# 512-column products for the small tiles, kept rotary tables and a split tail in an attention and expert block

## The chip, the cores and the metric

The kernel runs on one core of a Trainium2 chip. Its time is the device time of one launch in microseconds; the median of three runs before is 1562.0 us (1560.15 to 1563.43). A core has five engines with queues of their own: TensorE (PE; its weight loads are shown apart as PEld), VectorE (DVE), ScalarE (ACT), GpSimd (POOL) and SyncE (SP), which here only issues DMAs.

## What is computed

The block takes x of 2048 tokens by 256 features, normalises it, and adds attention and a mixture of experts to it. All of it is float32.

```python
xn = layernorm(x)
q, gate, k, v = split(xn @ w_qkv.T)          # 16 heads, 4 key/value heads, D = 128
q, k = rope(layernorm(q)), rope(layernorm(k))
attn = softmax(causal(q @ k.T / sqrt(D)))    # each k, v serves 4 heads
out = ((attn @ v) * sigmoid(gate)) @ w_o.T
w_tok = top-2 of 8 experts by softmax(xn @ w_router)
ffn = sum over experts of w_tok * (relu(xn @ w_fc) ** 2 @ w_proj)
result = x + out + ffn
```

## The kernel before

The work goes through four groups g (one key/value head and its HG = 4 query heads each) and within each through 16 tiles t of 128 tokens. Tile t attends to t + 1 key tiles, so tiles 0 to 7 are small and 8 to 15 large. Exact float32 products are made of three fp32r products each (`three`, L1279): high by high, high by low, low by high. So each operand that TensorE takes is first split: ScalarE copies it as the high part (`_hi`), VectorE subtracts for the low part (`_lo`).

For a tile the steps are: products `Q`, `KV`, `G` (gate); ScalarE's `q_take` and `kv_take` out of PSUM; the rotary part (`tables` on GpSimd from cosines and sines; `sumsq`, `same` on VectorE, `swap` and `rstd` on GpSimd, `rope_b` on VectorE); transposes `QT` and `KT` (L1339, L1343); the scores of each head in chunks of up to 512 keys; `max` on VectorE, `exp` on ScalarE into `probs`. Then the probabilities of a pair p of two heads are transposed, two key tiles i at a time: four blocks of 128 columns into a `pt_bank` (`turn_probs`, L1361), `p_hi` (L939), `p_lo` (L1219), and the value products `pv` of 256 columns into `o_bank`, a half of the bank for each pair. `turn_probs` step n waits for `p_lo` of step n - 2, since there are two `pt_bank`s. Then `o_take` per pair (L948), the transposed gate `GT` (L1382), `og` (L1234), `og_hi` (L957), `og_lo` (L1238), `OUT` (12 products, L1390) and `out_add` (L1243).

A tile with an odd number of key tiles ends with a half-wide step for each pair. The 23 expert slots run between the tiles from some 350 us on (`XS`, `H`, `Y`, with `xs_load`, `fc_load`, `pj_load` and `y_store` on SP; `y_store` waits for ScalarE's `y_take`).

At the start x is loaded in four parts of four tiles (`stats`, `x_rstd`, `norm`, then transposes `XT`, L1299, and `xT_lo`). The weights of a group come in two halves c, whose query part is centred (L1115 to L1119) and split (`wq_lo`, L1127); that of the gate is split by `wg_lo`.

What sets the order: `plan_program` (L334) places all steps on the five engines one by one, by assumed costs and a due time per step, from the tables `BEGIN` (one number for each tile and pair) and `DUE` (an offset for each kind of step). Each engine then works its list strictly in order, waiting on semaphores.

Of the kernel before, what the change touches and what calls it, by code (L numbers as in the profile page):

```python
# [38 lines left out]
P = 128  # L39
# [28 lines left out]
GATHER_AT, GATHER_EVERY = 440, 3  # L68
FILLS = (NSLOT + 1) // 2
ROUTE_PARTS = ((0, E), (E, E + E * E), (E + E * E, E + E * E + NSLOT), (E + E * E + NSLOT, 2 * E + E * E + NSLOT))  # L70
# [14 lines left out]
BEGIN = [26.59, 41.38, 29.62, 36.09, 25.65, 50.81, 47.59, 46.92, 64.18, 72.49, 75.23, 89.37, 102.35, 116.24,  # L85
# [10 lines left out]

DUE = {"qkv": -43.81, "rope": -12.53, "turn": -314.72, "v_lo": -91.35, "gate": 7.24, "inv": -214.95,
       "turn_gate": 4.73, "og": 4.02, "out": 10.53, "out_add": 1.16, "scores": -12.47, "max": -5.95,
       "exp": 18.26, "prob_step": 1.95, "pv": 7.99, "p_hi": -283.79, "p_lo": -1.72, "moe": 348.73,
       "moe_step": 36.0, "moe_evict": -19.57, "route": 89.48, "x1": 11.16, "x2": 38.95, "x3": 39.51,  # L100
       "logits": -17.39, "gate_w": -102.68, "scatter": 143.34, "next_w": -59.05, "wo": 575.69, "comb": 73.3,
       "window": 0.02}
# [18 lines left out]

def due_times():


    begin = {}
    for g in range(G):
        for t in range(T):
            for p in range(HG // 2):
                begin[g, t, p] = BEGIN[(g * T + t) * 2 + p]
    for g in range(G):  # L130
        begin[g, T, 0] = begin[g, T, 1] = begin[g + 1, 0, 0] if g + 1 < G else BEGIN[-1]
    return begin


def prob_order():


    return [(g, t, p, i) for g in range(G) for t in range(T) for p in range(HG // 2) for i in range((t + 2) // 2)]


def program_steps():
# [17 lines left out]
    for q in range(4):  # L159
        add("sp", ("x_load", q), 0.5, [], 0, 512)  # L160
        if q == 0:
# [3 lines left out]
        if q == 1:  # L165
# [9 lines left out]
    quarter = [0.0, DUE["x1"], DUE["x2"], DUE["x3"]]  # L175
    for q in range(4):
        add("dve stats", ("stats", q), 1.75, [("x_load", q)], quarter[q])
        add("pool x", ("x_rstd", q), 1.4, [("stats", q), ("pool_consts",)], quarter[q] - 5)
        add("dve norm", ("norm", q), 1.4, [("x_rstd", q)], quarter[q])
        for c in range(CT):  # L180
            i = 2 * q + c
            add("pe XT", ("XT", i), 0.44 if q else 1.06, [("norm", q), ("ident_load",)], quarter[q] + 2)
            add("act XT", ("xT_hi", i), 0.48, [("XT", i)], quarter[q] + 2)
            add("dve XT", ("xT_lo", i), 0.6, [("xT_hi", i)], quarter[q] + 2)
        add("pe L", ("L", q), 1.4, [("xT_lo", 2 * q + 1), ("wr_lo",)], quarter[q] + DUE["logits"])
        add("act L", ("logit_copy", q), 0.48, [("L", q), ("LT", q - 1) if q else None], quarter[q] + DUE["logits"])
        add("pe L", ("LT", q), 0.25, [("logit_copy", q)], quarter[q] + DUE["logits"] + 1)
        add("dve logit", ("route", q), 0.2, [("LT", q)], quarter[q] + DUE["logits"] + 1)
# [16 lines left out]
    for g in range(G):  # L205
# [20 lines left out]
        for t in range(T):  # L226
            b0, b1, b2 = begin[g, t, 0], begin[g, t, 1], begin[g, t + 1, 0]
            t1, t2 = tile_before(g, t), tile_before(g, t, 2)
            n_t = g * T + t
            if n_t >= 2:  # L230
                add("sp angles", ("angle_load", g, t), 0.45, [old(t2, "tables")], b0 + DUE["rope"] - 15, 64)
            add("pool rope", ("tables", g, t), 4.0, [old(t1, "rope_b"), old(t1, "same"), ("angle_load", g, t),
# [206 lines left out]
def build(nc, x, w_in, w_o, q_w, q_b, k_w, k_b, w_router, w_fc, w_proj, cos_sin, ident, mask_in, route_const, out):  # L439
# [9 lines left out]
    with ExitStack() as ctx:  # L449
# [3 lines left out]
        def sem(name):  # L453
            return ctx.enter_context(nc.semaphore(name))
# [1010 lines left out]
```

## Time and profile before

| | us |
|---|---|
| median of 3 runs | 1562.0 |
| the profiled execution | 1561.02 |
| its span, first to last instruction | 1559.2 |
| TensorE busy | 1508.5 |
| VectorE busy | 1310.9 |
| ScalarE busy | 1154.7 |
| GpSimd busy | 523.9 |
| end of the value products of tile 7, group 0 | 173.9 |
| end of the value products of tile 15, groups 0, 1, 2, 3 | 410.3, 805.9, 1191.9, 1551.4 |

Busy times are of one profiled execution. A matmul's end is modelled and overlaps the next one's start, so for a row of matmuls the distance between starts is their price, and TensorE's idle time is a lower bound of what it lost. The mean granted clock of TensorE is 0.996 of its full level.

### The profile page before, as it was taken

How to read it: one execution, taken by the hardware profiler on the slowest of the kernel's cores; microseconds unless marked ns; L12 is line 12 of the kernel's file. 1: busy time of each engine (PE TensorE's matmuls, PEld its weight loads, DVE VectorE, ACT ScalarE, POOL GpSimd, SP SyncE). 2: the span in 40 equal slices, each digit the busy share in tenths (PEclk: the TensorE clock that was granted, in tenths of full speed). 3: DMA queues.
4: the chain of work that ended last, by engine and by line, in shares of the span. 5: the costliest groups of instructions: out<-in, count | busy, mean ns of one | idle time of the engine just before them, and what ended most of it. 6: DMA issues, size and time to landing. Idle time of an engine off the chain costs nothing.

```text
span 1559.2 us, 29914 instructions
## 1 busy us (share of the span) xinstructions
PE 1508.5 (97%) x10589; PEld 1380.0 (89%) x10589; DVE 1310.9 (84%) x3011; ACT 1154.7 (74%) x3013; POOL 523.9 (34%) x726
## 2 busy tenths in 40 slices
PE   4999999999899999999999999999999999999998
PEld 3788999999899999999898999999998998899998
DVE  7999888787898888788789888887779988888875
ACT  3777777777778787787778777777777776776775
POOL 5544434320553222121046331221105535343200
PEclk9999999999999999999999999999999999999999
DMA  4400010001111000101211000110111101102000
GB/s 139 142 5 21 21 42 23 21 28 50 45 33 30 32 30 29 32 26 39 66 45 40 25 25 11 47 31 30 28 46 45 33 13 31 30 20 66 16 8 8
DMA packets 46646, 56.65 MB, mean 36 GB/s; under 512 B 4576, under 2 KB 43232, under 8 KB 46304
## 3 DMA queue, kind: packets, MB, share of 16 engines
q1 hardware_dynamic: 43424, 46.34, 9.5%
q0 software_dynamic: 3072, 8.39, 1.7%
q8 instruction: 84, 1.38, 0.4%
q14 instruction: 66, 0.54, 0.1%
HBM read 42.40 MB, written 18.35 MB: 39 GB/s over the span
## 4 chain that ended last, share of the span: by engine, by line
PE 74%; DVE 17%; ACT 5%; issue 2%; POOL 1%; DMA 1%; SPq 0%; DVEq 0%; ACTq 0%; POOLq 0%
PE bank L1286 39%; PE o_bank L1286 19%; PE pt_bank L1361 12%; DVE pT_lo L1219 3%; DVE neg_chunk_max L1205 2%; DVE t_same L1169 2%; DVE bank L1202 2%; PE bank L1339 1%; PE bank L1382 1%; DVE t_same L1165 1%; ACT probs L920 1%; DVE sumsq L1137 1%; DVE t_same L1153 1%; ACT gate L930 1%; ACT pT_hi L939 1%
## 5 line engine op out<-in xcount | busy, mean ns | idle before, releaser
L920 ACT ACTIVATE probs<-bank,neg_max 128x512 f32<-128x512 f32 (+3 forms) x640 | 399.8, 634 | 91.7 <-DVE neg_max L1212 57.6
L1219 DVE TENSOR_TENSOR pT_lo<-pt_bank,pT_hi 128x512 fp32r<-128x512 f32 (+1 forms) x576 | 368.7, 654 | 100.7 <-ACT pT_hi L939 96.8
L939 ACT ACTIVATE pT_hi<-pt_bank 128x512 fp32r<-128x512 f32 (+1 forms) x576 | 325.8, 578 | 131.3 <-PE pt_bank L1361 81.6
L1286 PE MATMUL o_bank<-pT_hi,v_hi 128*128 128x256 f32 x1088 | 333.7, 307 | 2.9 <-DVE pT_lo L1219 1.9
L1361 PE MATMUL pt_bank<-ident_f,probs 128*128 128x128 f32 x2176 | 315.2, 273 | 10.5 <-DVE pT_lo L1219 10.0
L785 POOL TENSOR_TENSOR t_swap<-qk_raw,table_swap 128x256 f32<-128x256 f32 (+1 forms) x256 | 135.4, 560 | 561.9 <-ACT t_same L889 560.9
L1286 PE MATMUL o_bank<-pT_hi,v_lo 128*128 128x256 f32 x1088 | 307.3, 282 | 0.0
L1286 PE MATMUL o_bank<-pT_lo,v_hi 128*128 128x256 f32 x1088 | 306.5, 282 | 0.0
L1205 DVE TENSOR_REDUCE neg_chunk_max<-bank 128x1 f32<-128x512 f32 (+1 forms) x384 | 244.8, 650 | 49.2 <-PE bank L1286 48.1
L1361 PEld LDWEIGHTS pt_bank<-ident_f,probs 128*128 128x128 f32 x2176 | 252.2, 140 | 36.0 <-DVE pT_lo L1219 13.5
L1286 PE MATMUL bank<-kT_hi,qT_hi 128*128 128x512 f32 (+3 forms) x640 | 244.0, 381 | 2.7 <-ACT probs L920 2.3
L1286 PE MATMUL bank<-kT_lo,qT_hi 128*128 128x512 f32 (+3 forms) x640 | 231.3, 361 | 0.0
L1286 PE MATMUL bank<-kT_hi,qT_lo 128*128 128x512 f32 (+3 forms) x640 | 231.1, 361 | 0.0
L1286 PEld LDWEIGHTS o_bank<-pT_hi,v_hi 128*128 128x128 f32 x1088 | 206.7, 190 | 9.9 <-DVE pT_lo L1219 4.7
L1286 PEld LDWEIGHTS o_bank<-pT_lo,v_hi 128*128 128x128 f32 x1088 | 207.2, 190 | 2.0
L1286 PEld LDWEIGHTS o_bank<-pT_hi,v_lo 128*128 128x128 f32 x1088 | 206.0, 189 | 0.0
L1286 PE MATMUL bank<-w_hi,xT_hi 128*128 128x512 f32 (+1 forms) x384 | 144.0, 375 | 3.9 <-DVE oT L1234 1.5
L1286 PEld LDWEIGHTS bank<-kT_hi,qT_hi 128*128 128x128 f32 x640 | 121.3, 189 | 19.3 <-ACT probs L920 6.9
L1286 PE MATMUL bank<-w_lo,xT_hi 128*128 128x512 f32 (+1 forms) x384 | 137.6, 358 | 0.0
L1286 PE MATMUL bank<-w_hi,xT_lo 128*128 128x512 f32 (+1 forms) x384 | 137.3, 358 | 0.0
L920 ACT ACTIVATION_READ_ACCUMULATOR probs<-bank,neg_max 128x1 f32 x640 | 137.1, 214 | 0.0
L1286 PEld LDWEIGHTS bank<-kT_hi,qT_lo 128*128 128x128 f32 x640 | 120.7, 189 | 17.0
(163 smaller groups left out, 2974.6 us busy)
## 6 DMA issues: line engine op xcount, KB each, us to landing
rows<-xs SPq DMA_DIRECT2D x23, 256.0 KB, 2.7
expert_raw<-in_w_fc SPq DMA_DIRECT2D x23, 256.0 KB, 3.0
expert_raw<-in_w_proj SPq DMA_DIRECT2D x23, 256.0 KB, 2.7
yb<-rows SPq DMA_DIRECT2D x23, 256.0 KB, 2.1
xs<-in_x SPq DMA_DIRECT2D x11, 512.0 KB, 4.9
w_raw<-in_w_in SPq DMA_DIRECT2D x7, 640.0 KB, 4.3
angles<-in_cos_sin SPq DMA_DIRECT2D x64, 64.0 KB, 1.9
acc<-in_x SPq DMA_DIRECT2D x4, 512.0 KB, 8.3
```

Of the source, the lines that this page charges most:

```text
L785: ins = pool.tensor_tensor(t_swap[:, heads, to], qk_raw[:, heads, of], table_swap[:, i:i + 1, to].to_broadcast([P, count, 64]), ALU.mult)
L920: act.activation(probs[:, u, h % 2, first:first + width], bank("scores", g, t, h, c)[:, 0:width], ACT.Exp, bias=neg_max[:, u, h % 2:h % 2 ...
L930: ins = act.activation(gh, gh, ACT.Identity, bias=inv, scale=inv)
L939: act.activation(pT_hi[:, n % PT_RING, 0:width], pt_bank[n % 2][:, 0:width], ACT.Copy)\
L1137: dve.tensor_reduce(sumsq[:], squares[:], AX.X, ALU.add).then_inc(sumsq_done, 1)
L1153: dve.tensor_tensor(t_same[:, 0:HG, :], qk_raw[:, 0:HG, :], table_same[:, 0:1, :].to_broadcast([P, HG, D]), ALU.mult).then_inc(same_done, 1)
L1169: ins = dve.scalar_tensor_tensor(rotated[:, h, :], t_same[:, h, :], rstd[:, h:h + 1], table_bias[:, h // HG, :], ALU.mult, ALU.add)
L1202: ins = dve.tensor_tensor_reduce(scores, scores, mask[:, CHUNK - width:CHUNK], 1.0, least, ALU.add, ALU.min, to)
L1205: ins = dve.tensor_reduce(to, scores, AX.X, ALU.min)
L1219: dve.tensor_tensor(pT_lo[:, n % PT_RING, 0:width], pt_bank[n % 2][:, 0:width], pT_hi[:, n % PT_RING, 0:width].bitcast(F32), ALU.subtract) ...
L1286: ins = pe.matmul(out_ap, s, m, start=(start and done == 1), stop=(stop and done == last))
L1361: ins = pe.transpose(pt_bank[n % 2][:, (2 * jj + hh) * P:(2 * jj + hh + 1) * P], probs[:, p, hh, j * P:(j + 1) * P], ident_f[:])
```

## The change

It has these parts.

- Tiles below SMALL = 8 handle all four heads together: a `turn_probs` step is one key tile of four heads, and `pv` is 512 columns wide, one step per key tile. `probs` is laid out by t % 2 there. `o_take` is one copy of 512 columns.
- The rotary tables are made by GpSimd in group 0 only; SP stores each (384 KB) to DRAM, and in groups 1 to 3 SP loads it back, into `made_tables` or into `norm_rows` (the table of norm weights, no longer needed), by t % 2.
- x is loaded in five parts, of 1, 3, 4, 4 and 4 tiles, and the first tile's two transposes go together.
- The last tile's `og`, `og_hi`, `og_lo` and `OUT` are done in two halves of two heads.
- `BEGIN` has 192 more numbers, three shifts for each tile, and nearly all numbers of `BEGIN` and `DUE` differ; the assumed costs follow the new widths. Scratch areas at the start lie elsewhere.

```diff
-GATHER_AT, GATHER_EVERY = 440, 3
+GATHER_AT, GATHER_EVERY = 428, 3
+SMALL = 8
+X_PARTS = ((0, 1), (1, 4), (4, 8), (8, 12), (12, 16))
...
-BEGIN = [26.59, 41.38, 29.62, 36.09, 25.65, 50.81, 47.59, 46.92, 64.18, 72.49, 75.23, 89.37, 102.35, 116.24,
+BEGIN = [15.02, 7.63, 57.3, 43.4, -9.53, -4.16, 15.06, 12.59, 36.85, 79.37, 35.75, 29.31, 53.04, 75.64, 82.97,
...
+def shift(g, t, k):
+    return BEGIN[2 * G * T + 1 + 3 * (g * T + t) + k]
...
+def head_groups(t):
+    return [range(HG)] if t < SMALL else [range(0, 2), range(2, 4)]
+def prob_blocks(t, i):
+    return [i] if t < SMALL else [j for j in (2 * i, 2 * i + 1) if j <= t]
+def prob_count(t):
+    return t + 1 if t < SMALL else (t + 2) // 2
...
+def probs_held(g, t, u):
+    if t < 2:
+        return (g - 1, T - 1, u, prob_count(T - 1) - 1) if g else None
+    if t < SMALL:
+        return g, t - 2, 0, prob_count(t - 2) - 1
+    if t == SMALL:
+        return g, SMALL - 2 + u, 0, prob_count(SMALL - 2 + u) - 1
+    return g, t - 1, u, prob_count(t - 1) - 1
...
+            if g == 0:
...
+                add("pool rope", table, 4.0, [old(t1, "rope_b"), old(t1, "same"), ("angle_load", g, t), ("ln_tables",),
+                                              ("table_store", t - 1) if t else None], b0 + DUE["rope"])
+                add("sp tables", ("table_store", t), 0.45, [table], 0, 384)
+            else:
+                table = ("table_load", g, t)
+                free = [("tables", 0, T - 1)] if (g, t) == (1, 0) else [old(t2 if n_t != T + 1 else t1, "rope_b")]
+                add("sp tables", table, 0.45, free + [("table_store", T - 1)], b0 + DUE["rope"] - DUE["table"], 384)
...
+        def rotary(g, t):
+            return made_tables if g == 0 or t % 2 else norm_rows
+        def wait_tables(w, g, t):
+            if g == 0:
+                w.wait_ge(tables_done, t + 1)
+            else:
+                w.wait_ge(tables_back[t % 2], 16 * (((g - 1) * T + t) // 2 + 1))
+        def prob_cols(t, h, first, width):
+            if t < SMALL:
+                return probs[:, t % 2, h * SMALL * P + first:h * SMALL * P + first + width]
+            return probs[:, h // 2, h % 2 * S + first:h % 2 * S + first + width]
...
+                elif kind == "table_store":
+                    w.wait_ge(tables_done, a[0] + 1)
+                    sp.dma_start(kept_tables[a[0]], made_tables[:]).then_inc(tables_kept, 16)
+                elif kind == "table_load":
...
+                        w.wait_ge(rotated_done, n - 1 if n > T + 1 else T)
+                    sp.dma_start(rotary(g, t)[:, 0:3], kept_tables[t]).then_inc(tables_back[t % 2], 16)
...
-                    width = 256 * min(2, t + 1 - 2 * i)
+                    width = P * len(head_groups(t)[p]) * len(prob_blocks(t, i))
...
-                    for jj in range(min(2, t + 1 - 2 * i)):
-                        for hh in range(2):
-                            j = 2 * i + jj
-                            ins = pe.transpose(pt_bank[n % 2][:, (2 * jj + hh) * P:(2 * jj + hh + 1) * P],
-                                               probs[:, p, hh, j * P:(j + 1) * P], ident_f[:])
+                    for k, (j, h) in enumerate((j, h) for j in blocks for h in heads):
+                        ins = pe.transpose(pt_bank[n % 2][:, k * P:(k + 1) * P], prob_cols(t, h, j * P, P), ident_f[:])
...
-                    for jj in range(min(2, t + 1 - 2 * i)):
-                        j, cols = 2 * i + jj, slice(2 * jj * P, 2 * (jj + 1) * P)
-                        ins = three(o_bank[:, 256 * p:256 * p + 256], [(v_hi[:, j, :], v_lo[:, j, :])],
+                    wide = P * len(head_groups(t)[p])
+                    for k, j in enumerate(prob_blocks(t, i)):
+                        cols = slice(k * wide, (k + 1) * wide)
+                        ins = three(o_bank[:, head_cols(t, p)], [(v_hi[:, j, :], v_lo[:, j, :])],
...
+                elif kind == "OUT_rest":
+                    g, t = LAST_TILE
+                    w.wait_ge(og_lo_done, g * T + t + 2)
+                    heads = range(HG // 2, HG)
```

Three places in the order of the instructions. The first is the start of VectorE's list. Before, `w_raw` and `probs` hold the two halves of the weights of group 0.

```order
L1023 TENSOR_SCALAR xn<-acc,probs 128x256 x4
L1127 TENSOR_TENSOR w_lo<-w_raw,w_hi 128x768
L1115 TENSOR_REDUCE head_sum<-probs 128x5
L1117 TENSOR_SCALAR head_mean<-head_sum 128x5
L1119 TENSOR_TENSOR probs<-probs,head_mean 128x640
L1029 TENSOR_TENSOR xT_lo<-bank,xT_hi 128x512
L1009 TENSOR_TENSOR wr_lo<-probs,wr_hi 128x16
L1029 TENSOR_TENSOR xT_lo<-bank,xT_hi 128x512
L1127 TENSOR_TENSOR w_lo<-probs,w_hi 128x768
```

Now, where `routing_rest` holds the second half of the weights:

```order
L1140 TENSOR_TENSOR wr_lo<-late_keys,wr_hi 128x16
L1145 BN_STATS late_keys<-acc 128x6 x3
L1148 BN_AGGR late_keys<-late_keys 128x2 x3
L1145 BN_STATS late_keys<-acc 128x6 x4
L1148 BN_AGGR late_keys<-late_keys 128x2 x4
...
L1257 TENSOR_TENSOR w_lo<-routing_rest,w_hi 128x768
...
L1154 TENSOR_SCALAR xn<-acc,late_keys 128x256 x11
L1288 TENSOR_TENSOR v_lo<-bank,v_hi 128x128
```

The 768-wide `w_lo` of the second half, for which the first Q product waits, stands behind the statistics of three more parts of x, and eleven normalisations stand between it and the first rotary step.

The second place is TensorE's list in an early small tile, tile 1 of group 0: transposition of probabilities and value products, before.

```order
L1361 MATMUL pt_bank<-ident_f,probs 128x128 x4
L1339 MATMUL bank<-ident_f,t_same 128x128 x4
L1286 MATMUL o_bank<-pT_hi,v_hi 128x256
L1286 MATMUL o_bank<-pT_lo,v_hi 128x256
L1286 MATMUL o_bank<-pT_hi,v_lo 128x256
```

Now the same tile, between scores of tile 2 (384 keys):

```order
L1421 MATMUL bank<-kT_hi,qT_lo 128x384
L1421 MATMUL o_bank<-pT_hi,v_hi 128x512
L1421 MATMUL o_bank<-pT_lo,v_hi 128x512
L1421 MATMUL o_bank<-pT_hi,v_lo 128x512
L1421 MATMUL bank<-kT_hi,qT_hi 128x384
```

Each key tile has three products of 512 columns in place of three for each of two pairs; the transposes of the tile's two key tiles, eight in a row, stand well ahead, with the rotary transposes and the projections of later tiles between.

The third place is the end of TensorE's list, before.

```order
L1286 MATMUL o_bank<-pT_hi,v_lo 128x256
L1382 MATMUL bank<-ident_f,gate 128x128 x4
L1286 MATMUL bank<-wo_hi,ogT_hi 128x256
L1286 MATMUL bank<-wo_lo,ogT_hi 128x256
L1286 MATMUL bank<-wo_hi,ogT_lo 128x256
```

Now:

```order
L1421 MATMUL bank<-wo_hi,ogT_hi 128x256
L1421 MATMUL bank<-wo_lo,ogT_hi 128x256
L1421 MATMUL bank<-wo_hi,ogT_lo 128x256
L1421 MATMUL o_bank<-pT_hi,v_hi 128x256
L1421 MATMUL o_bank<-pT_lo,v_hi 128x256
L1421 MATMUL o_bank<-pT_hi,v_lo 128x256
```

The gate's transposes have left the end, and the first six of the twelve OUT products stand ahead of the last six value products; six OUT products are left behind them.

## Rows read from the trace of the kernel before

**Rows 1.** The page: span, and TensorE's busy time (first entry, with share and instructions).

```profile
span 1559.2 us, 29914 instructions
...
PE 1508.5 (97%) x10589; PEld 1380.0 (89%) x10589; DVE 1310.9 (84%) x3011; ACT 1154.7 (74%) x3013; POOL 523.9 (34%) x726
```

**Rows 2.** Busy time by stretch; the first number is its length, then by engine.

```profile
core 0: us, PE busy (x) PEld busy (x) DVE busy (x) ACT busy (x) POOL busy (x), PEclk, DMA share, GB/s
0.00:20.00 20.00, 4.94 (x15) 2.63 (x16) 11.60 (x26) 5.50 (x9) 7.15 (x18) 1.00 0.68 200
20.00:60.00 40.00, 32.28 (x182) 24.61 (x182) 37.85 (x112) 24.29 (x67) 28.06 (x40) 0.96 0.29 98
60.00:120.00 60.00, 56.92 (x405) 50.72 (x404) 55.75 (x150) 43.64 (x124) 27.39 (x40) 1.00 0.16 55
...
410.00:548.00 138.00, 134.98 (x951) 124.61 (x950) 121.56 (x296) 108.90 (x289) 59.35 (x84) 0.99 0.11 34
...
1192.00:1327.00 135.00, 130.36 (x898) 118.34 (x896) 121.53 (x294) 103.52 (x281) 69.16 (x94) 1.00 0.09 25
1327.00:1551.00 224.00, 221.41 (x1570) 203.48 (x1569) 185.91 (x407) 158.80 (x415) 61.12 (x79) 1.00 0.08 25
```

**Rows 3.** The waits of all engines: us in total, times, longest us.

```profile
POOL table_same L769 <- DVE t_same L1169: 218.0, 59, 6.8
...
PE pt_bank L1361 <- DVE pT_lo L1219: 10.0, 16, 2.1
...
PE bank L1286 <- DVE xT_lo L1029: 8.9, 3, 6.1
...
PE bank L1339 <- DVE t_same L1169: 4.7, 8, 2.1
```

**Rows 4.** Timeline of TensorE near 1201 and 1223 us: start, length, instruction.

```profile
1201.12 0.28 PE L1286 MATMUL bank<-feat_hi,fc_hi 128*128 128x256 f32 x1
...
1202.44 0.28 PE L1286 MATMUL bank<-feat_hi,fc_lo 128*128 128x256 f32 x1
...
1222.76 0.40 PE L1286 MATMUL bank<-kT_hi,qT_hi 128*128 128x512 f32 x1
...
1224.86 0.28 PE L1286 MATMUL o_bank<-pT_hi,v_hi 128*128 128x256 f32 x1
```

**Rows 5.** VectorE's groups by shape: busy us, mean ns, idle before.

```profile
L1219 DVE TENSOR_TENSOR pT_lo<-pt_bank,pT_hi 128x512 fp32r<-128x512 f32 x512 | 343.6, 684 | 99.4 <-ACT pT_hi L939 95.8 <-issue 0.2
...
L1238 DVE TENSOR_TENSOR ogT_lo<-oT,ogT_hi 128x512 fp32r<-128x512 f32 x64 | 49.2, 768 | 2.8 <-ACT ogT_hi L957 2.5
...
L1219 DVE TENSOR_TENSOR pT_lo<-pt_bank,pT_hi 128x256 fp32r<-128x256 f32 x64 | 26.7, 417 | 1.3 <-ACT pT_hi L939 1.1
```

**Rows 6.** GpSimd's groups by shape; one of the five table operations.

```profile
L774 POOL TENSOR_TENSOR table_bias<-table_bias,t_swap 128x256 f32<-128x256 f32 x64 | 50.2, 784 | 5.0
```

**Rows 7.** Timeline of all engines, 0 to 45 us.

```profile
15.59 0.22 ACT L823 ACTIVATE wr_hi<-probs 128x16 fp32r<-128x16 f32 x1 [4.65 <-DMA routing_rest<-in_route_const]
...
17.25 0.96 DVE L1127 TENSOR_TENSOR w_lo<-probs,w_hi 128x768 fp32r<-128x768 f32 x1
...
19.79 0.63 PE L1286 MATMUL bank<-w_hi,xT_hi 128*128 128x512 f32 x1
...
21.56 1.37 DVE L1014 BATCH_NORM_STATS2 probs<-acc 128x6 f32<-128x256 f32 x4
...
24.32 1.38 DVE L1023 TENSOR_SCALAR xn<-acc,probs 128x256 f32<-128x256 f32 x4 [0.68 <-POOL probs L747]
...
31.26 2.64 DVE L1023 TENSOR_SCALAR xn<-acc,probs 128x256 f32<-128x256 f32 x4
...
31.49 0.63 PE L1339 MATMUL bank<-ident_f,t_same 128*128 128x128 f32 x4 [0.62 <-DVE t_same L1169]
```

**Rows 8.** Timeline of all engines, 1549.5 to 1560 us.

```profile
1551.40 0.38 ACT L948 ACTIVATE oT<-o_bank 128x256 f32<-128x256 f32 x1 [1.80 <-PE o_bank L1286]
...
1554.08 0.38 PE L1286 MATMUL bank<-wo_hi,ogT_hi 128*128 128x256 f32 x1 [2.28 <-DVE ogT_lo L1238]
...
1556.21 0.41 PE L1286 MATMUL bank<-wo_hi,ogT_lo 128*128 128x256 f32 x1
```

More of the change, by code:

```diff
@@ L157, in old @@
         return (kind, *tile, *rest) if tile is not None else None
-    for q in range(4):
-        add("sp", ("x_load", q), 0.5, [], 0, 512)
-        if q == 0:
+    for n, (first, last) in enumerate(X_PARTS):
+        add("sp", ("x_load", n), 0.5, [], 0, 128 * (last - first))
+        if n == 0:
             add("sp", ("ident_load",), 0.5, [], 0, 64)
@@ L174, in program_steps @@
     add("pool ln", ("ln_tables",), 3.4, [("ln_load",)], 0)
[L175 to L188, printed above, removed]
+    when = [0.0, DUE["x0"], DUE["x1"], DUE["x2"], DUE["x3"]]
+    for n, (first, last) in enumerate(X_PARTS):
+        tiles, at = last - first, when[n]
+        add("dve stats", ("stats", n), 0.44 * tiles, [("x_load", n)], at)
+        add("pool x", ("x_rstd", n), 1.4, [("stats", n), ("pool_consts",)], at - 5)
+        add("dve norm", ("norm", n), 0.35 * tiles, [("x_rstd", n)], at)
+        for i, c in turns_of(n):
+            width = tiles * P if c is not None else CT * P
+            add("pe XT", ("XT", i), 0.11 * width / P if n else 0.55, [("norm", n), ("ident_load",)], at + 2)
+            add("act XT", ("xT_hi", i), 0.07 + width / 1200, [("XT", i)], at + 2)
+            add("dve XT", ("xT_lo", i), 0.07 + width / 960, [("xT_hi", i)], at + 2)
+        if n:
+            q = n - 1
+            add("pe L", ("L", q), 1.4, [("xT_lo", 2 * n), ("wr_lo",)], at + DUE["logits"])
+            add("act L", ("logit_copy", q), 0.48, [("L", q), ("LT", q - 1) if q else None], at + DUE["logits"])
+            add("pe L", ("LT", q), 0.25, [("logit_copy", q)], at + DUE["logits"] + 1)
+            add("dve logit", ("route", q), 0.2, [("LT", q)], at + DUE["logits"] + 1)
     for k in range(4, ROUTE_STEPS):
@@ L280, in program_steps @@
                 for c, w in enumerate(chunks_of(t)):
[L281 removed]
+                    held_by = probs_held(g, t, t % 2 if t < SMALL else p)
+                    free = ("turn_probs", *held_by) if held_by else None
                     add("act S", ("exp", g, t, h, c), 0.24 + w / 1200,
                         [("max", g, t, h, len(chunks_of(t)) - 1), free, old(t2, "inv")], b + DUE["exp"])
[L284 to L285 removed]
+            for p, heads in enumerate(head_groups(t)):
+                last = prob_count(t) - 1
                 for i in range(last + 1):
[L287 removed]
+                    blocks = prob_blocks(t, i)
+                    four = len(heads) * len(blocks)
                     d = begin[g, t, p] + DUE["prob_step"] * i
@@ L1010, in _ @@
                 elif kind == "stats":
-                    q = a[0]
-                    w.wait_ge(x_in[q], 16)
-                    for t in range(4 * q, 4 * q + 4):
+                    first, last = X_PARTS[a[0]]
+                    w.wait_ge(x_in[a[0]], 16)
+                    for t in range(first, last):
                         dve.bn_stats(x_stats[:, t, :], acc[:, t, :]).then_inc(stats_done, 1)
-                    for t in range(4 * q, 4 * q + 4):
+                    for t in range(first, last):
                         w.wait_ge(stats_done, t + 1)
@@ L1018, in _ @@
                 elif kind == "norm":
-                    q = a[0]
-                    w.wait_ge(rstd_x_done, 2 * q + 2)
-                    w.wait_ge(means_done, 4 * q + 4)
-                    for t in range(4 * q, 4 * q + 4):
+                    first, last = X_PARTS[a[0]]
+                    w.wait_ge(rstd_x_done, 2 * a[0] + 2)
+                    w.wait_ge(means_done, last)
+                    for t in range(first, last):
                         dve.tensor_scalar(xn[:, t, :], acc[:, t, :], x_mv[:, t, 0:1], x_rstd[:, t:t + 1],
```

241 lines of the change are left out of this document (141 added, 100 removed), and 33 rows, old and new, of the table BEGIN.

## The prediction

> **What bounds the kernel now.** I read the page first, then the busy time by stretch, then the waits, then single stretches of the timeline. On the page TensorE is busy 1508.5 of 1559.2 us [rows 1], so 50.7 us of its time lies open at most by this measure. The stretches [rows 2] say where. Of the first 20 us TensorE is idle for 15.1, of the next 40 for 7.7, of 60 to 120 for 3.1: half of all idle time lies before tile 4 of the first group is through. VectorE in that stage is busy 37.9 of 40 and 55.8 of 60 us, so from 20 us on both engines run close to their limit and VectorE is the one waited for. The small tiles of the later groups look alike but milder: 3.0 us idle from 410 to 548 with VectorE at 88%, 4.6 us from 1192 to 1327 with VectorE at 90%. The large tiles (1327 to 1551) have TensorE at 99% and VectorE at 83%. The waits [rows 3] fit: TensorE's longest ones are for VectorE, at `pT_lo`, `xT_lo` and the rotary result `t_same`. GpSimd is waited for by nobody there, it waits itself (218 us of it before making tables). So three things can shorten the run: less TensorE work, less VectorE work in the small tiles and at the start, and a shorter head and tail.
>
> **512-wide value products.** Tiles 0 to 7 hold 36 key tiles in each of 4 groups. For each, six products of 256 columns become three of 512; that is 432 pairs. Nine 512-column products start between 1222.76 and 1224.86, 0.233 us apart, eleven of 256 between 1201.12 and 1202.44, 0.120 apart [rows 4]. A pair costs 0.240, the wide one 0.233: 432 x 0.0067 = 2.9 us less TensorE work. Rounding of the starts allows 1.5 to 4. The 2876 transposes stay, and fewer, longer runs of them cost nothing that I can find. I take 2.9, and all of it on the path, since TensorE is at 94% or more in all these stretches after 60 us. The Trainium skill (TensorE: Matmul & The Clock Gate, Back-to-back issue gap) gives N/2.4 + 2.5 ns for an isolated spacing; by it a pair would save 2.5 ns and the whole 1.1 us, which the measured spacings exceed.
>
> **Evictions.** A tile with an odd number of key tiles had two half-wide steps of `pT_lo`, 0.417 us each, and now has one full one at 0.684 [rows 5]. There are 16 such tiles, so VectorE saves 16 x (0.834 - 0.684) = 2.4 us, a quarter of it in each group. ScalarE saves as much and half of the `oT` copies of 32 tiles; it is at 74% and I cost that at nothing. If ScalarE were what paces a small tile, it would give a few tenths per tile more.
>
> **Kept tables.** In groups 1 to 3 GpSimd makes no tables: five operations of 0.74 to 0.78 us [rows 6], 48 times, some 184 us. Nobody waits for them [rows 3], so their going is worth nothing directly. What it can give is VectorE's own speed: `ogT_lo`, which reads SBUF twice, takes 0.768 us on the mean where `pT_lo` of the same width, with one operand in PSUM, takes 0.684 [rows 5]. That is 64 x 0.084 = 5.4 us for one operation; with the other SBUF operations of a tile I bound the sum by 15 us, and the tables are 184 of GpSimd's 524 busy us, so at most 5 us of VectorE time come free, in all stretches. Together with three quarters of the 2.4 us above that is under 7 us, of which the small tiles, where VectorE paces, hold about a third: I take 2.0 us (0 to 4). The Trainium skill (SBUF — State Buffer, Reading the diagram) has the same cause: a VectorE operation with two SBUF inputs and a GpSimd operation that reads SBUF lock each other out for a whole instruction. By it alone the gain per meeting would be up to a table operation's length, which the mean of `ogT_lo` does not reach.
> What comes instead is 16 stores and 48 loads of 384 KB on SP's queue, less 48 loads of angles. The loads stand among the expert loads and `y_store`, which waits for ScalarE; behind a late one VectorE's `t_same` would wait in order, and with it every `pT_lo` behind. I take 0: there are two table buffers and a load may go once the rotary step two tiles back is done, while before the tables could not start until the last one was. In the first group nothing is saved, and a table waits for the store before it.
>
> **The start.** Before, x comes in four parts; the first product for Q starts at 19.79, the first `QT` transposes at 31.49 [rows 7]. By the order now, one tile of x is normalised first and its gate product runs at once, but the statistics of the parts up to the fourth stand before the second `w_lo` of the query weights, and eleven normalisations before the first `sumsq`. Before, that `w_lo` was done at 18.2. Now, with `wr_lo` at about 14.5 (its constants came at 15.6 behind 384 KB more), 11 tiles of statistics at 0.44 (1.37 for four, and their aggregation) and the `w_lo` itself take it to about 20.5, so Q starts near 20.6, and `QT` comes 22.3 + 3.8 (eleven at 0.345) + about 6 = 32 to 34. TensorE is then about 2 us later and has 2 us less work behind it. VectorE, however, has by then done 4 more tiles of statistics and of normalisation, and its work up to the end of tile 7 of the first group is 3.4 us less by counting the order (0.6 of it the evictions, the rest moved to later, emptier stretches). VectorE being the one waited for, I take 1.0 us gain, with ends of -4 (gain) and +8 (loss).
>
> **The split tail.** Before, from the last `oT` copy at 1551.40 to the OUT product at 1554.08 are 2.7 us, and its twelve products start 0.19 apart on the mean instead of 0.12 [rows 8]. Halves of `oT`, `ogT_hi` and `ogT_lo` take about 0.27 less each, 0.8 together; six products fewer at the end save 1.2, but their 0.7 come earlier, into a stretch where TensorE is at 99%. Net 0.8 + 1.2 - 0.7 = 1.3 us (1 to 2.2).
>
> **Order.** All positions move, by a new table of due times. I counted TensorE's work between a transposition of probabilities and its value product: in the large tiles 3 of these distances are under 1.9 us of work (7 before), in the small ones 5 (3 before). That speaks for neither side, and I take 0.
>
> **Sum**, on the profiled execution's 1561.0 us (its span of 1559.2 and 1.8 around it, 1.0 below the median of 1562.0): 2.9 + 2.0 + 1.0 + 1.3 = 7.2, so 1553.8, and 1555 against the median. With every term at its good end it is 1548, at its bad end 1567 (which is rival c); most of the forecast's chance lies between 1550 and 1558.8.
>
> **Rivals.**
> (a) The new order closes waits as well. For it: 10.8 us of idle between 20 and 120 us [rows 2] and some 20 between there and the tail are order, not work. Halving both gives 13 to 15 us more: 1541. Against it: the short distances are as many as before.
> (b) VectorE takes the gain back. In the small tiles of the last group more VectorE work stands between tile 15 of the group before and tile 7 than before (by the order about 4 us, in all of groups 1 to 3 about 10), so TensorE's shorter work there only waits longer; 2.9 and 2.0 fall out: 1560.
> (c) Slower, at the start. The 11 normalisations run beside GpSimd and take 0.66 instead of 0.345 each, as four did at 31.26 [rows 7], 3.5 us; `QT` comes 2 us late with 2 us of work undone, 4 us; and as idle times go on, the granted clock, which was 0.96 on the mean of 20 to 60 us [rows 2], so partly at the lower of its two levels, 1.2 GHz, stays there for some 6 us more, 3 us. 1557 (without the start's gain and the tables') + 10.5 = 1567. It decides once tile 7 of the first group ends more than 8 us later than before; below that the other terms hold it at no change.
>
> **Chances.** Forecast 0.50, (a) 0.22, (b) 0.18, (c) 0.10. The range leaves out (c) and half of what lies beyond (a): 1541 to 1564. A measurement of this kernel tells some 0.2% (3.1 us) from no change: faster (below 1558.9) 0.72, same 0.18, slower 0.10.
>
> **What would show it.** In the new profile: `o_bank` products of 512 columns x432, their starts 0.233 apart; GpSimd busy near 340 us; `pT_lo` x560; no wait of VectorE for a table load over 1 us; TensorE's Q product near 20.6 us and `QT` at 32 to 34; the end of tile 7 of the first group, 173.9 us before, at 170 to 172; last `pv` to last instruction about 2 us shorter than 7.8. The forecast is wrong if TensorE's idle time in 20 to 120 us moves by more than 5 us either way, if VectorE waits for DMA, or if the clock falls below 0.9 in a stretch of 20 us that it did not before.

## The result: slower, by 1.5% in one kind of measurement and by 0.2% in the other

The changed kernel took 1585.5 us (1585.1 to 1586.7, 4 runs) beside 1561.9 for the kernel before: a ratio of 1.0151, 95% interval [1.0134, 1.0167], 23.6 us slower where 7 us faster were forecast. The kernels were measured in six groups, each on one chip and with the kernel before beside the others, and the groups are of two kinds. In the first kind the kernel before takes 1560.3 to 1561.9 us and the changed one is at 1.0151, twice; in the second, before takes 1555.8 to 1557.0 and the changed one is at 1.0022. I call them **kind I** and **kind II**; this first measurement and both its traces are of kind I.

The page of the changed kernel, where rows 1 stood for before:

```profile
span 1584.0 us, 28732 instructions
...
PE 1514.1 (96%) x10157; PEld 1359.5 (86%) x10157; DVE 1303.0 (82%) x2998; ACT 1148.3 (72%) x2967; POOL 345.9 (22%) x488
```

TensorE is idle for 69.9 us where it was idle for 50.7 [rows 1]. Its busy time by stretch in the changed kernel follows, in the columns of rows 2. The last four lines are the small tiles (0 to 7) of groups 1, 2 and 3 and the large tiles of group 3, between ends of value products:

```profile
0.00:20.00 20.00, 3.59 (x8) 2.11 (x8) 11.94 (x37) 5.18 (x9) 7.55 (x21) 1.00 0.77 226
20.00:60.00 40.00, 35.35 (x200) 26.67 (x200) 38.08 (x109) 27.14 (x73) 29.62 (x41) 1.00 0.35 116
60.00:120.00 60.00, 57.49 (x352) 49.31 (x351) 55.33 (x149) 45.50 (x126) 26.74 (x40) 0.97 0.26 86
401.90:534.40 132.50, 128.83 (x806) 112.74 (x807) 118.21 (x289) 106.37 (x276) 25.78 (x40) 1.00 0.19 55
788.70:928.60 139.90, 131.40 (x803) 112.20 (x801) 118.12 (x287) 103.92 (x267) 28.90 (x43) 1.00 0.17 50
1187.00:1322.20 135.20, 128.65 (x788) 112.34 (x788) 118.33 (x292) 101.86 (x269) 29.10 (x44) 0.99 0.15 45
1322.20:1578.50 256.30, 237.21 (x1624) 215.55 (x1621) 193.05 (x420) 165.63 (x430) 50.44 (x62) 0.97 0.11 32
```

The same stretch of group 2 in the kernel before:

```profile
805.90:938.40 132.50, 130.68 (x922) 120.66 (x922) 119.98 (x292) 106.71 (x289) 60.79 (x86) 1.00 0.10 29
```

Two places stand out. The small tiles of group 2 have 8.5 us of TensorE idle, before 1.8. The large tiles of the last group take 256.3 us with 19.1 idle; before they took 224.7, with 2.6 idle in 1327 to 1551 [rows 2]. Up to 1322 us the changed kernel was 4.5 us ahead: the value products of tile 7 of group 3 end at 1322.2 us, before at 1326.7.

What waits there, in TensorE and ScalarE, 1440 to 1584 us of the changed kernel (total, times, longest):

```profile
PE bank L1421 <- ACT probs L1050: 11.2, 4, 3.6
PE pt_bank L1494 <- DVE pT_lo L1349: 5.9, 2, 5.5
...
ACT pT_hi L1069 <- remote: 13.2, 5, 5.8
```

"Remote" means that the trace knows no releaser. The longest of these, in the timeline of all engines:

```profile
1548.80 0.60 PE L1494 MATMUL pt_bank<-ident_f,probs 128*128 128x128 f32 x4
...
1549.39 0.94 POOL L942 DMA_INDIRECT gathered_rows<-yb,place  x1 [0.30 <-issue]
...
1550.36 0.69 DVE L1335 TENSOR_REDUCE neg_chunk_max<-bank 128x1 f32<-128x512 f32 x1 [1.49 <-remote]
1550.64 0.95 POOL L942 DMA_INDIRECT gathered_rows<-yb,place  x1 [0.30 <-issue]
1551.89 0.95 POOL L942 DMA_INDIRECT gathered_rows<-yb,place  x1 [0.30 <-remote]
1554.68 1.08 ACT L1069 ACTIVATE pT_hi<-pt_bank 128x512 fp32r<-128x512 f32 x2 [5.81 <-remote]
1555.31 0.69 DVE L1349 TENSOR_TENSOR pT_lo<-pt_bank,pT_hi 128x512 fp32r<-128x512 f32 x1 [4.26 <-ACT pT_hi L1069]
...
1556.06 0.69 PE L1494 MATMUL pt_bank<-ident_f,probs 128*128 128x128 f32 x2 [5.50 <-DVE pT_lo L1349]
```

The transposes that `pT_hi` needs are through by 1549.4; ScalarE starts it at 1554.68. From 1551.1 us on only GpSimd works, on the last of a run of eight gathers (`gathered_rows`, one each 1.25 us), and from 1552.8 to 1554.7 no engine does. The other stalls lie in such runs too, or within 3 us behind one: 1457 to 1467, 1481 to 1491, 1516 to 1526, 1543 to 1553.

Behind the stalls TensorE runs slower too. The busy time of engines and the granted clock (the third number from the end) during and after two of them:

```profile
1485.00:1490.00 5.00, 2.27 (x18) 2.02 (x17) 2.76 (x7) 1.27 (x3) 3.78 (x5) 0.99 0.36 105
1490.00:1495.00 5.00, 2.88 (x10) 2.00 (x9) 1.86 (x4) 2.49 (x7) 3.77 (x6) 0.50 0.18 52
...
1550.00:1556.00 6.00, 0.56 (x5) 0.32 (x3) 1.38 (x3) 1.08 (x2) 2.23 (x3) 0.89 0.26 80
1556.00:1562.00 6.00, 5.94 (x24) 5.27 (x25) 3.39 (x8) 0.74 (x2) 0.00 (x0) 0.54 0.00 0
```

The clock is at its lower level, half of the full one, for most of 1490 to 1495 and of 1556 to 1562 us; 512-column products start 0.43 us apart there (1557.40 to 1557.83) instead of 0.23.

Why the gathers come in runs is in SyncE's timeline. They wait for the store of the last expert slot (`y_store` 22). Of before, then of the changed kernel:

```profile
1281.87 0.38 SPq L716 DMA_DIRECT2D yb<-rows  x1
```

```profile
1273.94 0.37 SPq L846 DMA_DIRECT2D yb<-rows  x1
...
1454.38 0.37 SPq L846 DMA_DIRECT2D yb<-rows  x1
```

In the changed kernel 1273.94 is slot 21's store; slot 22 missed the small tiles. The planner allows steps other than scores one bank among the large tiles, and slot 22 came through 173 us later than before. By then nearly all marks of `pt_filled` that space the gathers had passed (the last few passed before their run began), so only the buffer of four tiles limited them: eight, four tiles' sums, eight again.

### The profile page after: what moved, and what is told of

The parts are those of the page before. It is cut to its first block, busy times and chain, and to the rows that moved or that the text cites. A ratio compares the mean times of both kernels' runs of the same rounds, so it can differ in the third digit from the quotient of the medians.

```text
span 1584.0 us, 28732 instructions
## 1 busy us (share of the span) xinstructions
PE 1514.1 (96%) x10157; PEld 1359.5 (86%) x10157; DVE 1303.0 (82%) x2998; ACT 1148.3 (72%) x2967; POOL 345.9 (22%) x488
## 4 chain that ended last, share of the span: by engine, by line
PE 52%; issue 27%; DVE 11%; POOL 4%; ACT 4%; another core or an unknown queue 1%; DMA 1%; SPq 0%; DVEq 0%; POOLq 0%; ACTq 0%
PE bank L1421 27%; PE o_bank L1421 14%; PE pt_bank L1494 9%; POOL t_swap L916 2%; DVE t_same L1299 2%; ACT probs L1050 1%; POOL rstd L925 1%; DVE pT_lo L1349 1%; DVE bank L1332 1%; DVE neg_chunk_max L1335 1%; PE bank L1474 1%; DVE t_same L1295 1%; ACT pT_hi L1069 1%; PE bank L1519 1%
## 5 line engine op out<-in xcount | busy, mean ns | idle before, releaser
L1421 PE MATMUL o_bank<-pT_hi,v_hi 128*128 128x256 f32 (+1 forms) x944 | 307.6, 326 | 3.2 <-DVE pT_lo L1349 3.1
L1421 PE MATMUL o_bank<-pT_hi,v_lo 128*128 128x256 f32 (+1 forms) x944 | 283.0, 300 | 0.0
L1421 PE MATMUL o_bank<-pT_lo,v_hi 128*128 128x256 f32 (+1 forms) x944 | 282.4, 299 | 0.0
L1421 PEld LDWEIGHTS o_bank<-pT_hi,v_hi 128*128 128x128 f32 x944 | 179.9, 191 | 10.4 <-DVE pT_lo L1349 5.0
L1421 PEld LDWEIGHTS o_bank<-pT_hi,v_lo 128*128 128x128 f32 x944 | 179.1, 190 | 6.2
L1421 PEld LDWEIGHTS o_bank<-pT_lo,v_hi 128*128 128x128 f32 x944 | 180.4, 191 | 3.7
L916 POOL TENSOR_TENSOR t_swap<-qk_raw,norm_rows 128x256 f32<-128x256 f32 (+1 forms) x96 | 52.1, 575 | 570.5 <-ACT t_same L1019 570.5
L916 POOL TENSOR_TENSOR t_swap<-qk_raw,made_tables 128x256 f32<-128x256 f32 (+1 forms) x160 | 85.7, 566 | 402.8 <-ACT t_same L1019 402.4
```

Source lines behind the costliest of these rows:

```text
L916: ins = pool.tensor_tensor(t_swap[:, heads, to], qk_raw[:, heads, of], rotary(g, t)[:, 1, i:i + 1, to].to_broadcast([P, count, 64]), ALU.mult)
L1421: ins = pe.matmul(out_ap, s, m, start=(start and done == 1), stop=(stop and done == last))
```

## The experiments

Times are ratios to the kernel before measured beside it on the same chip, with their 95% intervals. Each kernel is the changed one with an edit, or the one before with an edit.

**1. Which of three: bursts (A), the late slot's own work (B), the large tiles' order (C)?** First the slot early: the planner takes the steps of slot 22 (`URGENT` lists its products, copies and splits) ahead of all else.

```
             if step[0] in MOE_EVICTS:
                 when = start + DUE["moe_evict"]
+            if step[0] in URGENT and step[1] == NSLOT - 1:
+                when = -1000.0
```

> The changed kernel, with the last expert slot (number 22) taken ahead of all else as soon as its inputs are there; every position up to its transposes stays. In the changed kernel its result is stored at 1454 us and the 32 gathers of expert rows go out in four bursts of eight between 1457 and 1553 us; here, by the order, the store should come near 1310 us and the gathers should be spread over the large tiles as in the kernel before. Theory A (the bursts of gathers stop ScalarE) and theory B (the late slot's own work and the late sums are what costs) both expect the 24 us that TensorE lost between 1440 and 1556 us back, most of them: 1560 us, within 6. Theory C (the large tiles are slower by the new order as such) expects 1578 us or more.

Kind II: 1.0045 [1.0031, 1.0058]. The store came at 1290.88. Read against the changed kernel of kind I this looked like 16 us back; within kind II, as it turned out, it is 4 us lost.

> The changed kernel with its last expert slot early, so that the gathers are spread over the large tiles, a second time. Where before takes 1557 us it was 1.0045. Where before takes 1561.7: if bursts are what costs, 1.002 to 1.006 against 1.015 for the changed kernel; if every gather costs alike, 1.012 or more.

Kind I: 1.0029 [1.0019, 1.0038], so there it does give 19 us back. C falls for kind I; A and B both expected this.

Bursts without a late slot, every other engine's order kept: each eight gathers moved to where their first one stood in GpSimd's list.

```
+    for q in range(4):
+        eight = ahead[8 * q:8 * q + 8]
+        at = order["pool"].index(eight[0])
+        order["pool"] = order["pool"][:at] + eight + [s for s in order["pool"][at:] if s not in eight]
```

> The kernel with the last slot early, and the order of TensorE, ScalarE and VectorE as in that one to the last instruction; only GpSimd's 32 gathers stand in four runs of eight, one behind the other, each run where its first gather stood. Theory A expects ScalarE to stand still for 3 to 6 us in each run of eight, as in the changed kernel: 12 to 20 us more than with the last slot early. Theory B expects the same time as with the last slot early, within 4 us.

Kind II: 1.0137 [1.0121, 1.0152], 14 us over the early slot with its gathers less bunched. The number is A's, the cause is not: no wait on "remote" is in it. VectorE's waits, 1290 to 1573 us:

```profile
DVE t_same L1305 <- POOL t_swap L926: 10.7, 2, 5.4
```

GpSimd's swap for the rotary step stood behind eight gathers, which take 10 us. VectorE works its list in order and waited for the swap, and so did every `pT_lo` behind it.

> The changed kernel with the last slot early and the 32 gathers in four runs of eight, a second time. It was 1.0137 where before takes 1556 us, 14 us over the kernel with the gathers spread, and there by GpSimd's rotary steps standing behind the gathers. Where before takes about 1561 us that comes again and the stalls of the bursts with it: 1.020 or more against 1.003 with the gathers spread. If the bursts stop the engines only when they stand late, 1.012 to 1.015.

Kind I: 1.0156 [1.0139, 1.0173], 20 us over the early slot there (14 in kind II), less than the 1.020 of the expectation. The two waits for GpSimd's swap come again (10.0 us), and "remote" ones appear, as in the second run of gathers (1330 to 1339 us):

```profile
1338.22 0.60 ACT L1079 ACTIVATE pT_hi<-pt_bank 128x512 fp32r<-128x512 f32 x1 [2.39 <-remote]
1338.53 0.94 POOL L952 DMA_INDIRECT gathered_rows<-yb,place  x1 [0.30 <-issue]
1339.65 0.69 DVE L1375 TENSOR_TENSOR oT<-bank,oT 128x512 f32<-128x512 f32 x1 [5.19 <-remote]
```

The late slot in the kernel before, its transposes, `H` and `Y` held back in the planner until steps of tiles 9, 11 and 13:

```
-        add("pe MOE", ("Y", m), 1.44, [("hid_lo", m), ("pj_lo", m)], at)
+        add("pe MOE", ("Y", m), 1.44, [("hid_lo", m), ("pj_lo", m)] + ([("turn_probs", *prob_steps[530])] if m == NSLOT - 1 else []), at)
```

> The kernel before, with its last expert slot held back until tiles 11 to 13 of the last group, so that its store comes near 1460 us instead of 1282 and the 32 gathers behind it follow as fast as they can; nothing else of the change is in it. Theories A and B expect 20 to 28 us more than before: 1582 to 1590 us, with ScalarE idle for reasons that the trace does not name in each burst of gathers. Theory C expects no more than 6 us: at most 1568 us.

Kind II, where the changed kernel has no "remote" waits either, so A could not show itself: 1.0114 [1.0099, 1.0129], 18 us, less than A and B said. The store came at 1460.78 and the planner stacked the sums of four tiles on VectorE:

```profile
1495.60 4.12 DVE L1270 SCALAR_TENSOR_TENSOR acc<-gathered_rows,p,acc 128x256 f32<-128x256 f32 x8
1499.75 1.89 DVE L1205 TENSOR_REDUCE neg_chunk_max<-bank 128x1 f32<-128x512 f32 x3
```

TensorE waited 6.0 us for the `pT_lo` behind them. Late sums are theory B's way, so in another plan a late slot can cost by it. In kind I this kernel was not measured.

**2. Do the gathers stop the engines?** SyncE issues 32 plain loads of the same bytes at the same points, in place of GpSimd's gathers by index (the rows added are not the right ones):

```
+                        w.wait_ge(y_stored, 16 * NSLOT)
+                        w.wait_ge(pt_filled, GATHER_AT + GATHER_EVERY * (2 * t + j) + 1)
...
+                        sp.dma_start(gathered_rows[:, j, t % 4, :], yb[(2 * t + j) * P:(2 * t + j + 1) * P]).then_inc(gathered[q], 16)
...
                 elif kind == "gather":
+                    continue
```

> The changed kernel in its own order, with the last slot as late as it is; in place of GpSimd's 32 gathers by index SyncE issues 32 plain loads of 128 rows each, of the same bytes, into the same buffers at the same points (so that the rows added at the end are not those that the router chose). Theory A in its narrow form (gathers by index, issued by GpSimd, are what stops ScalarE) expects 14 to 20 us less than the changed kernel: 1565 to 1571 us. Theory A in its wide form (any 128 KB loads that close together do it) and theory B expect 1585 us, within 4.

> The changed kernel with its 32 gathers by index replaced by plain loads of the same bytes at the same points (the rows added are not the right ones), a second time. Where before takes 1557 us it was 1.001. Where before takes 1561.7: if the gathers are what stops the engines, 0.997 (the 1561.7 itself would hold some 4 us of such stalls); if it is the late slot or anything else in the large tiles, 1.010 to 1.015.

Kind II: 1.0010 [1.0001, 1.0019]. Kind I: 0.9981 [0.9972, 0.9991], with the slot as late as ever, so B falls as well. Its large tiles in kind I, for the 256.3 us with 237.21 busy above:

```profile
1320.40:1550.30 229.90, 229.06 (x1624) 210.16 (x1621) 191.70 (x420) 165.15 (x430) 20.00 (x30) 1.00 0.12 36
```

So in kind I the gathers by index cost the changed kernel 1.0151 - 0.9981 = 0.0170, 26.5 us. The two rows split it: 18.3 us are more idle time of TensorE (19.1 against 0.8), and 8.2 us are more busy time for the same 1624 products, at a mean granted clock of 0.97 instead of 1.00. Nearly a third of the cost is the clock behind the stalls. Whether the index or GpSimd's issuing matters is not separated: no run has plain loads issued by GpSimd. The same replacement in the kernel before:

> The kernel before with its 32 gathers as plain loads issued by SyncE at nearly the same points (the rows added at the end are not the right ones). If gathers by index cost time even where they stand apart, through GpSimd's rotary steps that stand behind them or otherwise, it is 3 to 8 us faster than before (ratio 0.995 to 0.998). If only bursts cost anything, it is 1.000.

> The kernel before with plain loads in place of its 32 gathers (the rows added are not the right ones), a second time. Where before takes about 1561 us: 0.997, if its own gathers hold the 4 to 5 us by which it is longer there; 1.000 if that has another source. Where before takes 1557: 0.9994, as the first time.

Kind II: 0.9994 [0.9985, 1.0004]; kind I: 0.9965 [0.9953, 0.9978]. So the 32 gathers of the kernel before cost 5.5 us in kind I and next to nothing in kind II. That accounts for the difference between the two levels of before.

These gathers are not evenly spread either. In the trace of before the first seven go out 1.25 us apart (1284.59 to 1292.24), the next quarter begins with five (1326.90 to 1332.02). The end of the first run, in the timeline of before:

```profile
1289.96 0.40 PE L1286 MATMUL bank<-kT_hi,qT_lo 128*128 128x512 f32 x1
...
1293.17 0.76 DVE L1202 CUSTOM_DVE_ANT_0 bank<-bank,mask,neg_chunk_max 128x512 f32<-128x512 f32 x1 [2.08 <-PE bank L1286]
...
1294.02 0.69 ACT L920 ACTIVATE probs<-bank,neg_max 128x512 f32<-128x512 f32 x1 [3.73 <-DVE neg_max L1202]
...
1296.53 0.66 PE L1361 MATMUL pt_bank<-ident_f,probs 128*128 128x128 f32 x4 [2.09 <-DVE pT_lo L1219]
```

The scores that VectorE masks were written by 1290.4, and it was free from 1291.1 on, but it starts at 1293.17; in kind II it starts on them without a wait. TensorE is idle for 2.1 us in 1278 to 1300 and for 1.6 us in 1320 to 1350, against 0.0 and 0.2 us in kind II, and 0.0 and 0.3 in kind I with plain loads. The releaser that the profile names there had long been done, so the "remote" waits do not count all stalls.

Every second gather left out of the changed kernel (the sums read the first expert's rows twice):

```
                     w.wait_ge(acc_done, acc_number["comb", t // 4 * 4 - 1])
+                    if j:
+                        continue
```

> The changed kernel with every second gather left out (the rows of the second expert are not fetched; the sums read the first expert's rows twice and take as long), all else as it is, the late last slot included: bursts of four gathers, 5 us long, instead of eight. If the stall comes of gathers that stand close together for longer than some 5 us, as the first stall in each burst of eight came only after the fifth gather or so, it is gone: 1.001 of before, as with plain loads. If each gather costs the same, half of the 22 us between the changed kernel and the one with plain loads is left: 1.008.

> The changed kernel with every second gather left out, so bursts of four in place of eight (the sums read the first expert's rows twice), a second time. Where before takes about 1561 us: if the stalls come only in long bursts, 0.998 to 1.001, as with plain loads; if each gather costs alike, 1.006 to 1.008. Where before takes 1557: 1.002, as the first time.

Kind II: 1.0018 [1.0009, 1.0028]; kind I: 1.0007 [0.9997, 1.0016]. Half the gathers, in runs of four, take away 85% of the cost in kind I (0.0144 of 0.0170): long runs cost, not each gather alike.

**3. Is it the chip?** Both kernels unchanged again:

> The changed kernel once more, unchanged, beside kernels whose times are compared with it. Ratio to before 1.015, as in its first measurement. In the large tiles of the last group ScalarE should again stand still in each burst of gathers for reasons that the trace does not name (18 us of TensorE's waiting between 1463 and 1556 us). If that was a matter of one chip or one execution and not of the kernel, the ratio here is under 1.008.

> The kernel before once more, for a profile from the same chip as the others of this call: ratio 1.000, within 0.001.

> The changed kernel a third time. It stood at 1.015 of before where before took 1561.9 us, and at 1.002 where before took 1557.0 us. If it is a matter of the chip, it is one of these two here: 1.015 beside a before of about 1562, 1.002 beside 1557. Anything between would speak for a third cause.

The second time, in kind II, the changed kernel has 1.0022 [1.0013, 1.0032] and before 1.0001 [0.9991, 1.0011]; the third time, in kind I, the changed one has 1.0151 [1.0136, 1.0167]. So there are two kinds and nothing between. But the chip does not tell them apart, as far as its number goes: both of these measurements were on chip number 1. (Kind II came on 5 and 1, kind I on 1, 6 and 11; the first measurement has no number.) Whether one number is the same chip each time is not known, so the kind may belong to a chip or to a state that a chip is in.

In kind I the seven "remote" waits of ScalarE come at the same instructions with the same lengths (5.85 for 5.81, 3.05 for 3.06); in kind II the same runs of eight gathers go out at the same 1.25 us and no such wait exists. All 20 profiles, 12 of kind I and 8 of kind II, differ in one more thing, the transfers that GpSimd issues. Of kind II, then kind I (time to landing last):

```profile
gathered_rows<-yb,place POOLq DMA_INDIRECT x32, 2.7
```

```profile
gathered_rows<-yb,place POOLq DMA_INDIRECT x32
```

In kind I the profile sees no landing of these. The chain of the changed kernel's page there names "another core or an unknown queue" for 1% of the span, which fits; it is no explanation.

**4. The change's parts in the old order.** The kernel before with the split tail alone; with the kept tables alone (TensorE's, ScalarE's and VectorE's order to the last instruction that of before); with both. The tail's edit is the change's own code for `LAST_TILE`; the tables' is its `table_store` and `table_load`, put into the old lists:

```
+    order["pool"] = [step for step in order["pool"] if step[0] != "tables" or step[1] == 0]
...
+        timed.append((gone + 1.0, -1, ("table_load", n // T, n % T)))
```

> The kernel before with the split tail alone: the last tile's product of the gate, its two casts and the output product go in two halves, all else and its order as before. By the prediction's term 1.3 us faster (1 to 2.2): ratio 0.9992, and the time from the last value product to the last instruction 1 to 2 us shorter. If half-wide steps cost as much as they save, 1.000.

> The kernel before with the kept tables alone: GpSimd makes the rotary tables in the first group only, SyncE stores them and loads them back in groups 1 to 3; the order of TensorE, ScalarE and VectorE is that of before to the last instruction. By the prediction 1 to 3 us faster (ratio 0.998 to 0.9995), all of it from VectorE's operations with two SBUF inputs going faster where GpSimd no longer makes tables. If GpSimd's work never held VectorE up where it paces, 1.000; if VectorE or GpSimd waits for table loads, over 1.001 and the waits show it.

> The kernel before with the kept tables alone, a second time. It was 0.9965 beside a before of 1561.7 us. Where before takes 1557 us: the same 5 us (0.9966) if the gain is VectorE's shorter operations; less, 0.998 to 1.000, if part of it was that gathers and tables no longer meet on GpSimd.

> The kernel before with the split tail and the kept tables together, in the order of before: two of the change's parts without its 512-wide products, its start and its new order. The parts alone stood at 0.999 and 0.9965 of before. If they add up, 0.9955 (7 us), whichever way the last slot's gathers behave on this chip.

All in kind I; what they give in kind II was not measured. Tail: 0.9990 [0.9981, 0.9999], 1.6 us. Tables: 0.9965 [0.9953, 0.9977] and again 0.9965 [0.9952, 0.9978], 5.5 us. Both: 0.9950 [0.9936, 0.9963], 1553.1 us: **0.5% below before, and so faster than both kernels**. How the tables alone pay, on their page and in VectorE's groups (rows 5 for before):

```profile
PE 1506.5 (97%) x10589; PEld 1379.5 (89%) x10589; DVE 1301.9 (84%) x3011; ACT 1153.8 (74%) x3013; POOL 347.0 (22%) x486
```

```profile
L1277 DVE TENSOR_TENSOR ogT_lo<-oT,ogT_hi 128x512 fp32r<-128x512 f32 x64 | 45.5, 711 | 2.8 <-ACT ogT_hi L996 2.5
```

VectorE does the same 3011 instructions in 9.0 us less (8.2 the second time), with GpSimd 177 us less busy. `ogT_lo`, with both operands in SBUF, falls from 768 to 711 ns; `pT_lo` of the same width, with one in PSUM, stays at 684. The Trainium skill (SBUF — State Buffer, section "SBUF: two separate sides") has a lock between an operation with two SBUF inputs and one of GpSimd that reads SBUF; the trace agrees. It also says there that ScalarE and TensorE never wait on anyone for SBUF, so the stalls of kind I would have to be something else. No run here tells what.

## Why the prediction was wrong, step by step

**The step that failed is "Order ... I take 0".** I judged the new table of due times by the distances between `turn_probs` and `pv` alone. Two things were in it. First the last expert slot, a chain of loads, products and a store that 32 gathers and 16 sums wait for. The planned order had its `y_store` far back, in tile 12 of the last group, and I did not look. In kind I the runs of gathers behind it cost 26.5 us where those of before cost 5.5; the step had 0 for it, and the difference is 21 of the 23.6 us. I could have seen the runs coming in the order. I could have seen their price too: the longest of TensorE's waits for `pT_lo` in rows 3, 2.1 us, is the one at 1296.53 behind before's own run of seven, and I did not look at what stood there.

Second, the order costs elsewhere. With gathers out of play on both sides, changed against before is 0.9981 / 0.9965 = 1.0016 in kind I and 1.0010 / 0.9994 = 1.0016 in kind II. All else of the change is 2.5 us of loss, alike in both, where I had 7.2 of gain. Tail and tables alone bring 7.8 in the old order; so start, 512-wide products and new order together lose some 10. (The 7.8 was measured with gathers in and the 2.5 without, so this is good to a few us.) TensorE's idle time points at a place. Small tiles of groups 1 to 3, with plain loads in the changed order, then tail and tables in the old order:

```profile
400.50:532.90 132.40, 128.81 (x806) 112.69 (x807) 118.06 (x289) 106.33 (x276) 26.28 (x40) 1.00 0.18 55
...
787.30:927.00 139.70, 131.49 (x802) 112.25 (x800) 118.02 (x287) 103.93 (x267) 28.84 (x43) 1.00 0.17 51
...
1185.40:1320.40 135.00, 128.44 (x788) 112.23 (x787) 118.33 (x292) 101.68 (x268) 29.03 (x44) 0.99 0.15 45
```

```profile
411.10:546.00 134.90, 132.65 (x945) 122.95 (x944) 118.20 (x294) 108.05 (x289) 28.52 (x44) 1.00 0.18 54
...
804.00:936.20 132.20, 130.93 (x923) 120.77 (x922) 118.30 (x292) 106.62 (x290) 26.84 (x40) 1.00 0.18 52
...
1189.20:1321.60 132.40, 129.08 (x898) 118.00 (x896) 118.52 (x293) 103.06 (x281) 35.11 (x48) 1.00 0.16 48
```

3.6 + 8.2 + 6.6 = 18.4 us idle against 2.3 + 1.3 + 3.3 = 6.9, with VectorE's work the same to 0.3 us in each. That is rival (b)'s place and direction, at 11.5 us and not at some 5, but not its cause: (b) had more work of VectorE in these stretches, and there is none. Some of the work of TensorE stands in other stretches in the changed order, so the 11.5 is no exact share of the 10. Which waits of the order make it was not taken apart by a run, and that cause stays open.

**Tables and evictions, 2.0 (0 to 4): mechanism right, size off.** The tables alone gave 5.5. I bounded VectorE's relief by 5 us (9.0 measured), and took a third of it as on the path; 5.5 of 9.0 is more than half. The table loads on SyncE at 0 were right: VectorE has no wait for one.

**Tail, 1.3 (1 to 2.2): right.** 1.6 alone, and from the last `pv` to the last instruction 5.5 us instead of 7.8. The rows of the changed kernel that answer to rows 8:

```profile
1578.58 0.38 ACT L1079 ACTIVATE oT<-o_bank 128x256 f32<-128x256 f32 x1 [2.27 <-PE o_bank L1421]
...
1580.38 0.38 PE L1421 MATMUL bank<-wo_hi,ogT_hi 128*128 128x256 f32 x1 [1.84 <-DVE ogT_lo L1370]
...
1581.07 0.28 PE L1421 MATMUL bank<-wo_hi,ogT_lo 128*128 128x256 f32 x1
```

The chain from the copy to OUT is 1.8 us instead of 2.7, and six products follow in 0.7.

**512-wide products, 2.9 (1.5 to 4): open.** Their instructions are 432 fewer [10157 for 10589] and start 0.23 us apart, as said; but such a step cannot be put into the old order, so no run isolates its gain. With plain loads in kind I, at the same mean clock of 0.998, TensorE is busy for 1504.1 us in the changed kernel and for 1504.5 in the kernel before, so little of the 2.9 shows in busy time.

**Start, 1.0: fair.** Q began at 20.75 us (said: 20.6), `QT` at 32.32 (32 to 34), and the idle time of TensorE in 0 to 60 us fell from 22.8 to 21.1. The value products of tile 7 of the first group ended at 167.5 us instead of 173.9, earlier than the 170 to 172 I gave, and the large tiles of that group kept it (401.9 for 410.3). Rival (c), the only slower case, had its mark at 8 us later: it did not happen. The kernel was slower by a mechanism that was in none of my cases, and what I listed to watch (GpSimd near 340: 345.9; `pT_lo` x560: 528 and 32; idle in 20 to 120 us within 5: 3.6 less) came out as said while the time was 24 us off. One of its signs of being wrong did appear: the granted clock is 0.83 in 1480 to 1500 and in 1550 to 1570 us, and 1.00 before in 1480 to 1500; it followed from the stalls. Nothing on that list looked at the end of the last expert slot.

## What to carry to other kernels

When all positions move, look first at the longest chains that end in something many instructions wait for (here a store, 32 gathers, 16 sums), not only at the tight loop's distances: where does each link stand now, and what spaced the work behind it? Gathers by index on GpSimd are an engine's time in order (1.25 us each), and a run of them holds up GpSimd's other work and, in one kind of measurement here, ScalarE and VectorE too, with TensorE behind them; keep them apart, and measure again another time, on another chip if you can, before you trust a ratio within 2%. Look in the trace of the kernel that you have for the thing that the change will make longer. Parts that can go into the old order should be tried there: two of this change's parts gave 0.995 without the rest.

## What the runs showed of the hardware that was not expected

In kind I, runs of eight gathers by index, 1.25 us apart, delay starts on ScalarE and VectorE whose inputs are ready by up to 5.3 us, and before's run of seven by 2.1; with runs of four (and half the gathers) 85% of the cost is gone, and with plain loads of the same bytes all of it. The granted clock falls to half behind the longer stalls, and that is 8.2 of the 26.5 us. In kind II none of this appears. Why the two kinds differ stays open; the chip's number does not tell them apart. GpSimd's table work slowed VectorE by 9.0 us in 1311, almost twice what I had bounded from the means of two operations.
